# Riding dt's columns on z's projection and spreading short work over the steps of an attention and state-space kernel

## The reference, cut to what matters

```python
q = einsum('dc,bcn->bnd', wq, xf) + bq;  k = ... ;  v = ...          # layer 0, d = 32
x1 = gamma * einsum('bcn,bmn->bcm', v, softmax(q @ k)) + x
u = layernorm(x1 as tokens) * norm_g + norm_b                         # layer 1
zxbcdt = einsum('bld,ed->ble', u, in_w)                               # 772 rows of in_w
z, xBC, dt = zxbcdt[..., :256], zxbcdt[..., 256:768], softplus(zxbcdt[..., -4:] + dt_bias)
xs, B, C = split(silu(causal_conv4(xBC) + conv_b))
state = state * exp(dt_t * A) + (dt_t * x_t) outer B_t;  y_t = state @ C_t + Dp * x_t
y = y * silu(z);  y = y * rsqrt(mean(y * y) + eps) * rms_w
out = y @ out_w.T;  result = x1 + out * gate(mean(out))
```

## Time and profile before

| | |
|---|---|
| median of 3 runs | 3138.42 us (3137.31 to 3141.98) |
| the profiled execution | 3134.2 us |
| its span, first to last instruction | 3132.1 us |
| TensorE busy | 2969.5 us |
| VectorE, ScalarE, GpSimd busy | 2038.2, 1922.7, 2006.3 us |
| mean granted clock of TensorE, share of full speed | 0.982 |

### The profile page before, as it was taken

The page is one execution under the profiler, slowest core; times in us unless marked ns, Lnnn a source line. Parts: engine busy times, 40 slices in busy tenths (PEclk is TensorE's granted clock), DMA queues, the critical chain, the costliest instruction groups (busy, mean ns, idle before and its releaser), DMA issues. The chain is left out here.

```text
span 3132.1 us, 63156 instructions
## 1 busy us (share of the span) xinstructions
PE 2969.5 (95%) x21208; PEld 2322.8 (74%) x21208; DVE 2038.2 (65%) x3417; ACT 1922.7 (61%) x3742; POOL 2006.3 (64%) x3087
## 2 busy tenths in 40 slices
PE   6899999999999999999999999999999999999984
PEld 3767777777777777777777777777778777777763
DVE  5556666666766676676676666676666667676654
ACT  2555666666656666666665666666666666666652
POOL 2446666667756666666776656666676767777763
PEclk9999999999999999999999999999999999999996
DMA  4111111121321121222220122211221011111121
GB/s 123 49 44 33 45 58 54 35 61 40 100 71 65 58 84 48 89 77 70 83 95 30 57 85 65 78 66 64 73 90 36 30 63 62 56 63 50 55 95 67
DMA packets 101970, 200.99 MB, mean 64 GB/s; under 512 B 18480, under 2 KB 41392, under 8 KB 97264
## 3 DMA queue, kind: packets, MB, share of 16 engines
q1 hardware_dynamic: 98192, 195.08, 18.6%
q10 hardware_dynamic: 3456, 1.86, 0.2%
HBM read 131.21 MB, written 64.75 MB: 63 GB/s over the span
## 5 line engine op out<-in xcount | busy, mean ns | idle before, releaser
L723 POOL TENSOR_TENSOR p_lo<-p,p_hi 128x512 f16<-128x512 f32 x1024 | 1219.6, 1198 | 836.8 <-ACT p_hi L886 709.1
L879 ACT ACTIVATE p<-p_et 128x512 f32<-128x512 f32 x1024 | 612.2, 598 | 638.4 <-PE p_et L1138 591.7
L1156 PE MATMUL acc<-v_hi,p_hi 128*128 128x257 f16 x4096 | 955.3, 274 | 4.0 <-DVE work L1464 3.8
L1158 PE MATMUL acc<-v_lo,p_hi 128*128 128x256 f16 x4096 | 952.9, 273 | 0.0
L1420 DVE TENSOR_REDUCE maxes<-p_mx 128x1 f32<-128x1024 f32 x508 | 620.2, 1221 | 500.0 <-PE p_mx L1117 499.8
L886 ACT ACTIVATE p_hi<-p 128x512 f16<-128x512 f32 x1024 | 644.4, 629 | 10.0
L1164 PE MATMUL acc<-v_hi,p_lo 128*128 128x257 f16 x4096 | 623.0, 274 | 16.7 <-POOL p_lo L723 16.7
L1156 PEld LDWEIGHTS acc<-v_hi,p_hi 128*128 128x128 f16 x4096 | 399.8, 98 | 125.0 <-issue 54.6
L1158 PEld LDWEIGHTS acc<-v_lo,p_hi 128*128 128x128 f16 x4096 | 400.9, 98 | 118.6 <-issue 50.4
L1164 PEld LDWEIGHTS acc<-v_hi,p_lo 128*128 128x128 f16 x4096 | 400.0, 98 | 69.9 <-POOL p_lo L723 17.6
L1138 PE MATMUL p_et<-qs,kst 98*128 98x256 f16 x2048 | 393.2, 273 | 12.4 <-ACT p L879 11.7
(11 more groups left out here) (213 smaller groups left out, 4163.5 us busy)
## 6 DMA issues: line engine op xcount, KB each, us to landing
work<-rows_d SPq DMA_DIRECT2D x32, 1024.0 KB, 5.1
xin<-in_x_dram SPq DMA_DIRECT2D x48, 512.0 KB, 5.2
xr<-in_x_dram SPq DMA_DIRECT2D x32, 512.0 KB, 3.7
x_d<-x1c SPq DMA_DIRECT2D x31, 512.0 KB, 3.0
og_d<-og SPq DMA_DIRECT2D x29, 512.0 KB, 2.7
mix_x<-x_d SPq DMA_DIRECT2D x25, 512.0 KB, 4.7
mix_o<-og_d SPq DMA_DIRECT2D x24, 512.0 KB, 5.6
out_dram<-mix_o SPq DMA_DIRECT2D x24, 512.0 KB, 2.8
```

Of the source, the lines that this page charges most:

```text
L723: e.tensor_tensor(p_lo[:, n % RING, :], p32[:, n % P32S, :], p_hi[:, n % RING, :], ALU.subtract).then_inc(lo_pool, 1)
L879: e.activation(p32[:, n % P32S, :], p_et[:, :], ACT.Exp).then_inc(exp_done, 1)
L1156: e.matmul(acc[:, t, 0:C + 1], p_hi[:, r, at:at + P], v_hi[:, 2 * k + kk, 0:C + 1], start=(k == 0 and kk == 0), stop=False)
L1158: e.matmul(acc[:, t, 0:C], p_hi[:, r, at:at + P], v_lo[:, 2 * k + kk, :], start=False, stop=False, skip_group_check=True)
```

## The change

The weights of z and dt lie side by side in `inz_sb`, and a fill of z covers one chunk of 128 tokens with 260 columns, 256 of z and 4 of dt. There are four such fills, at steps 10, 11, 13 and 15. The separate fill of dt is gone. VectorE adds the bias of dt for one chunk at a time, together with z's product. The rest of dt's chain, the decays and their loads are 4 to 5 steps later. `zt` has two buffers. The root mean square's three Newton rounds are spread over steps 23, 24 and 25. `max_parts` stands ahead of `stage_b` and `stage_a` in its step.

```diff
-K_X1T, K_UT, K_DT, K_DAT, K_CUM, K_YT, K_OUT = 3, 9, 10, 21, 23, 30, 0
+K_X1T, K_UT, K_DT, K_DAT, K_CUM, K_YT, K_OUT = 3, 9, 15, 25, 27, 30, 0
-K_Z = (22, 24)
-K_XSB = (25, 27, 28, 29)
+K_Z = (10, 11, 13, 15)
+K_XSB = (26, 27, 28, 29)
...
-        inT_sb = sb("inT_sb", [P, CH, 2 * C + 2 * NST + NH])
+        inT_sb = sb("inT_sb", [P, CH, CONVD])
+        inz_sb = sb("inz_sb", [P, CH, C + NH])
...
-                   (inT_sb[:, :, :], inT.rearrange("(h p) n -> p h n", p=P)),
+                   (inT_sb[:, :, :], inT[:, C:C + CONVD].rearrange("(h p) n -> p h n", p=P)),
+                   (inz_sb[:, :, 0:C], inT[:, 0:C].rearrange("(h p) n -> p h n", p=P)),
+                   (inz_sb[:, :, C:C + NH], inT[:, C + CONVD:C + CONVD + NH].rearrange("(h p) n -> p h n", p=P)),
...
-            def root_mean(g):
-                e.wait_ge(rms_guess, g + 1)
-                newton(rw).then_inc(rms_ready, 1)
+            def root_mean(g, part):
+                if part == 0:
+                    e.wait_ge(rms_guess, g + 1)
+                ins = newton(rw, 1)
+                if part == 2:
+                    ins.then_inc(rms_ready, 1)
...
-                    if K == K_RMS + 1:
-                        root_mean(g)
+                    if K_RMS + 1 <= K < K_RMS + 4:
+                        root_mean(g, K - K_RMS - 1)
...
-                if K == K_DAT - 2:
+                if K == K_DAT - 1:
                     e.wait_ge(dt_ready, g + 1)
                     wait(e, filled, n_filled(("dAT", g - 1, 0)) if g else 0)
                     e.activation(dA16[:, :], dtt[:, 7, :], ACT.Exp).then_inc(dA_done, 1)
...
+                for t in range(QT):
+                    if K == K_Z[t]:
+                        key = ("z", g, t)
                         e.wait_ge(filled, n_filled(key))
+                        wait(e, y_ready, (g - 1) * QT)
+                        e.activation(zt[g % 2][:, t, :], bank(key)[:, 0:C], ACT.Tanh, scale=0.5).then_inc(ztanh_done, 1)
...
-                elif name == "dt":
+                elif name == "z":
                     e.wait_ge(uT_done, 2 * g + 2)
                     o = begin(key)
-                    for t in range(QT):
-                        for h in range(CH):
-                            mm = e.matmul(o[:, t * NH:(t + 1) * NH], uT[:, h, t * P:(t + 1) * P],
-                                          inT_sb[:, h, C + CONVD:C + CONVD + NH], start=(h == 0), stop=(h == CH - 1))
-                    mm.then_inc(filled, 1)
-                elif name == "z":
-                    o = begin(key)
-                    for t in range(2):
-                        for h in range(CH):
-                            mm = e.matmul(o[:, t * C:(t + 1) * C], uT[:, h, (2 * i + t) * P:(2 * i + t + 1) * P],
-                                          inT_sb[:, h, 0:C], start=(h == 0), stop=(h == CH - 1))
+                    for h in range(CH):
+                        mm = e.matmul(o[:, 0:C + NH], uT[:, h, i * P:(i + 1) * P], inz_sb[:, h, :],
+                                      start=(h == 0), stop=(h == CH - 1))
                     mm.then_inc(filled, 1)
...
+                for t in range(QT):
+                    if K == K_Z[t]:
+                        key = ("z", g, t)
+                        e.wait_ge(ztanh_done, QT * g + t + 1)
+                        if t == 0:
+                            wait(e, dt_ready, g)
+                        v.tensor_tensor(dtt[:, 0, t * NH:(t + 1) * NH], bank(key)[:, C:C + NH], dtb[:, :], ALU.add)
+                        v.scalar_tensor_tensor(zt[g % 2][:, t, :], zt[g % 2][:, t, :], 1.0, bank(key)[:, 0:C],
+                                               ALU.add, ALU.mult).then_inc(zs_done, 1)
+                if K == K_DT:
+                    e.drain()
+                    v.scalar_tensor_tensor(dtt[:, 1, :], dtt[:, 0, :], -1.0, dtt[:, 0, :], ALU.mult, ALU.max)\
+                        .then_inc(dtabs_ready, 1)
+                    v.tensor_scalar(dtt[:, 3, :], dtt[:, 0, :], 0.0, None, ALU.max)
+                if K == K_DT + 2:
+                    e.wait_ge(dtexp_done, g + 1)
+                    v.tensor_scalar(dtt[:, 4, :], dtt[:, 2, :], 2.0, None, ALU.add)
...
+                    if K % STEPS == (K_PARTS if n >= STEPS else K_PARTS_FIRST) and n // STEPS + 1 < NHALF:
+                        max_parts(n // STEPS + 1)
                     if h < NHALF and K % STEPS == (K_QR if n >= STEPS else K_QR_FIRST):
                         query_rows(h)
```

More of the change, by code:

```diff
@@ L130, in fills_at @@
             out += [("uT", A, 0), ("uT", A, 1)]
-        if K == K_DT:
-            out += [("dt", A, 0)]
         if K == K_DAT:
@@ L136, in fills_at @@
             out += [("cumT", A, 0)]
-        for r in range(2):
-            if K == K_Z[r]:
-                out += [("z", A, r)]
+        for t in range(QT):
+            if K == K_Z[t]:
+                out += [("z", A, t)]
         for c in range(QT):
@@ L268, in conv_attention_mamba_kernel @@
         yT = work[:, 4096:5120].rearrange("p (h n) -> p h n", h=CH)
-        zt = work[:, 5120:6144].rearrange("p (t c) -> p t c", t=QT)
+        zt0 = work[:, 5120:6144].rearrange("p (t c) -> p t c", t=QT)
         dAb = work[:, 6144:8192]
+        zt = [zt0, sb("zt1", [P, QT, C])]
         xin = [sb(f"xin{r}", [P, CH, BLK]) for r in range(2)]
@@ L756, in decays, with newton @@
                                 ALU.mult).then_inc(Sd_ready, 1)
-            def newton(w):
-                for _ in range(3):
+            def newton(w, steps=3):
+                for _ in range(steps):
                     e.tensor_tensor(w[:, 1, :], w[:, 3, :], w[:, 3, :], ALU.mult)
@@ L951, in stage_a @@
                         e.activation(th[:, m % 2, :], cv, ACT.Tanh).then_inc(tanh_done, 1)
-                for r in range(2):
-                    if K == K_Z[r]:
-                        key = ("z", g, r)
+                for t in range(QT):
+                    if K == K_Z[t]:
+                        key = ("z", g, t)
                         e.wait_ge(filled, n_filled(key))
-                        wait(e, y_ready, g * QT)
-                        e.activation(zt[:, 2 * r:2 * r + 2, :], bank(key)[:, :].rearrange("p (t c) -> p t c", t=2),
-                                     ACT.Tanh, scale=0.5).then_inc(ztanh_done, 1)
+                        wait(e, y_ready, (g - 1) * QT)
+                        e.activation(zt[g % 2][:, t, :], bank(key)[:, 0:C], ACT.Tanh, scale=0.5).then_inc(ztanh_done, 1)
                 for c in range(QT):
@@ L1531, in stage_a @@
                         v.memset(xbc[:, :, 0:HALO], 0.0).then_inc(halo_done, 1)
-                for r in range(2):
-                    if K == K_Z[r]:
-                        key = ("z", g, r)
-                        e.wait_ge(ztanh_done, 2 * g + r + 1)
-                        v.scalar_tensor_tensor(zt[:, 2 * r:2 * r + 2, :], zt[:, 2 * r:2 * r + 2, :], 1.0,
-                                               bank(key)[:, :].rearrange("p (t c) -> p t c", t=2), ALU.add, ALU.mult)\
-                            .then_inc(zs_done, 1)
+                for t in range(QT):
+                    if K == K_Z[t]:
+                        key = ("z", g, t)
[13 more added lines that the diff above has]
+                    v.tensor_scalar(dtt[:, 4, :], dtt[:, 2, :], 2.0, None, ALU.add)
+                    e.drain()
+                    v.reciprocal(dtt[:, 5, :], dtt[:, 4, :])
+                    e.drain()
+                    v.tensor_tensor(dtt[:, 4, :], dtt[:, 2, :], dtt[:, 5, :], ALU.mult).then_inc(dtz_ready, 1)
                 if K == K_DAT:
@@ L1634, in step @@
                 if s < G:
-                    if K % STEPS == (K_PARTS if n >= STEPS else K_PARTS_FIRST) and n // STEPS + 1 < NHALF:
-                        max_parts(n // STEPS + 1)
                     if K == K_BN:
```

31 lines of the change are left out of this document (6 added, 25 removed).

## The result

The changed kernel takes 3171.52 us (median of 4 runs, 3169.69 to 3174.78) against 3137.86 of the kernel before on the same chip (4 runs, 3133.5 to 3141.98): a ratio of 1.0108, 95% interval 1.0093 to 1.0123. It is slower by 34 us, where 37 us less were forecast. The profiled execution has a span of 3172.7 us, 40.6 more than before; about 7 of these 40.6 are spread between executions, since the profiled one lies 3.7 us under the median before and 3.3 over it after.

The account below looks back on a forecast made before the run. TensorE's list was taken to set the pace. The terms, from -52.7 for dt's fill to +17 for new waits at steps 22 to 26, sum to -37 us: 3097 profiled, 3101 median; 8-in-10 range 3076 to 3122.

Parts of the forecast that it names:

- an end stage longer by over 8 us: Sign of being wrong: the stage behind the last tile grows by more than 8 us.
- the shorter slots: Sign of being right: slots without projections become shorter by about 1.2 us.
- The fill of dt: Step 10: removing dt's separate fill takes 1.70 us a slot, 52.7 us in all, off TensorE.
- Dt's matmuls are hidden: Rival at dt's fill: weights load under other matmuls, only 2 us are won, 3152 us; chance 0.02.
- The fills of z: Four fills for two on TensorE: 1.8 us for added columns, 3.2 us for changes between matmul kinds.
- Steps 10 to 21: Steps 10 to 15 save 2.7 us in all through shorter waits; steps 17 to 21 cost 3 us.
- The 3 us at steps 17 to 21: TensorE waits 0.1 us a slot for the exponential at step 21, since dt's VectorE work delays a tap.
- Steps 22 to 26: New wait for the exponential at step 26: 10 us, plus 7 in special slots, less 9.0 of v fill.
- GpSimd as 0: Steps 18 to 26: moved series and split rounds keep every `p_lo` in time, so GpSimd costs 0.
- GpSimd becomes the bound: Rival at steps 18 to 27: series and rounds come too late, about 3205 us; chance 0.05.
- The end: Behind the last tile: dt's later chain through series, load and scan costs 2 us, from -6 to +8.
- The decay rows: Made 4 steps later; slack between load landing and scan falls from 21 to 10 us, so hidden.

Follow-up runs that it names:

- e13: Changed kernel with two of a slot's 32 `p_lo` (tiles 24 and 25) replaced by a memset of 4 columns: 3114.81 us.
- e2: Changed kernel with the three root mean square rounds in one piece again at step 23: 3171.94 us.
- e10: e8 with the three root mean square rounds in one piece again, at step 22: 3191.4 us.
- e7: Changed kernel with the last block kept in its old order (own dt fill, z at steps 22 and 24): 3157.47 us.
- e5: Changed kernel with the root mean square's guess at step 21, last square at step 20, rounds at steps 22 to 24: 3120.94 us.
- e8: Changed kernel with both the guess at step 21 and the old order for the last block: 3111.23 us.
- e11: e8 with `max_parts` behind `stage_b` and `stage_a` again, as in the kernel before: 3097.56 us.
- e14: Changed kernel with only `max_parts` put behind `stage_b` and `stage_a` again: 3133.11 us.

## Why the prediction was wrong

The bound, the terms for TensorE's own work and the place of the new wait were right. What failed is the length of VectorE's short operations at steps 22 to 24, the clock behind a wait, and the price of the chain in the end stage. One of the prediction's signs of being wrong came, an end stage longer by over 8 us; of its signs of being right, the shorter slots did not (slot 25 takes 89 us).

**The fill of dt: right.** Step 10 takes 27.2 us less in 30 slots with a z chunk of 0.87 in dt's place, so dt cost 1.78 us a slot; 1.70 was counted. *Dt's matmuls are hidden* is refuted: by that rule step 10 would have become longer. The prediction also says that at 25 ns a matmul "the change would take only some 12 us off"; that is dt's term alone (31 x 0.4), and its whole sum would then be about +3. The section of the Trainium skill that it takes the 25 ns from (page TensorE: Matmul & The Clock Gate, section Back-to-back issue gap) gives them for a matmul by itself, and says that in a stream with a weight load for each matmul the load counts too; each of dt's 512 had one, and the trace has 0.106 us.

**The fills of z: right.** Four chunks cost 3.51 us a slot against 3.45 for two fills before, 1.7 us in all; 5.0 was counted. VectorE's 256-column passes took 0.41, as the earlier trace rows let expect.

**Steps 10 to 21: right, some us too dear.** `cb` waits for z's product 3.7 us in 3 slots, and the idle time of steps 15 and 16 went from 7.6 us to 0.5. The 3 us at steps 17 to 21 did not come (0.4 us, once).

**Steps 22 to 26: this step failed.** The place was right (the scores of step 26, for the exponential, behind Tanh and third tap), the direction too, and the size wrong: 17 us of new waits less 9 won, where 75 were measured. The count set the third tap's end 6.1 us behind the start of step 22. With the two `p_lo` away (e13) it is 6.2, and TensorE's waits for the exponential at step 26 come to 9.4 us, close to the 10 that I counted; steps 22 to 27 then take 455.0 us, 15 above the 439.7, where I had counted 8. What the count left out is that the 0.17 us of a small operation of VectorE (the guess's rows of before, above) hold only while no `p_lo` runs beside it. The trace of before showed this in other places, where I took no row: the subtraction that makes `mparts`, 2 elements a partition, took 0.44 us on average there and 0.16 in slot 25. I moved `max_parts` in the list as a harmless 0.9 us and did not ask what it and the series would put side by side.

**The clock: no term at all.** In 13 of the 30 slots TensorE ran at half the clock behind this wait, 3.4 us in twelve and 6.8 in one. There it made a wait of 1.9 us cost 3.6.

**GpSimd as 0: right here for the wrong reason.** I argued that splitting the rounds keeps `p_lo` in time. The time is the same without it (e2), because another wait hid it; in e10, where that wait is gone, my argument holds and is worth 80 us. The rival *GpSimd becomes the bound* did not come as priced, its rounds stayed at 0.35 us each; but GpSimd did cost the time, through VectorE.

**The end: too small.** +14 (e7 gives it back: -14.0; e5 to e8: -9.7), counted as +2 within -6 to +8. That dt comes late behind z and the convolution was right; the chain that I priced behind it, through the decays' load and the scan, was not the one that ended last. The 7.8 us between scan and `cb` were no room to be eaten: the two are still 6.6 us apart. What TensorE waited for is what I named in one sentence and gave no price: root mean square and output of the block before, behind GpSimd's series. The rounds start 12.8 us later, the output fill 10.1, and at half the clock it takes 2.8 more.

**The decay rows: right.** In slot 25 the load is issued at 2498.51 and read at 2514.59, 16 us later.

On the span, the forecast of -37 and the measured +40.6 differ by 77.6 us: 67 in steps 22 to 27 (75 against 8), 12 in the end stage, and 2 the other way in all the rest.

## What to carry to other kernels

When work leaves the bounding engine, list for the stretch it left every operation of the other engines up to the next thing awaited, and price a small one by what its kind costs where it meets GpSimd, not by a place where it stood alone: an operation of 0.17 us on VectorE can cost what is left of GpSimd's operation beside it. The mean of the group is no guard if all of it stood alone, as the guess's did before (0.17); the subtraction's 0.44 was the hint. An order that looks neutral (which of two short pieces of VectorE work goes first) was worth 38 us, more than half of it in the steps concerned through the clock, and the same edit was worth 80 us or nothing (the rounds) and 50 or 4 (the guess), depending on what else was late; so parts of a change are worth testing one by one and again on the repaired version. The last block, behind which nothing is hidden, may need an order of its own.

## What the runs showed of the hardware

A `tensor_scalar` or cast of VectorE over a few elements in SBUF takes 0.16 to 0.17 us alone and up to 1.15 us in the changed kernel where a `p_lo` of GpSimd has begun before it (1.10 for the guess's first operation in slot 25 of e11), and ends when that one does. So does the subtraction of `max_parts`, which has two SBUF inputs: 0.16 against up to 1.15. The taps, which read PSUM and one SBUF tensor, are not touched, 755 ns on average before and after, and the small reduction ahead of `max_parts`' other three takes 161 in both, beside a `p_lo` or not. The Trainium skill has the rule (page SBUF — State Buffer, section Who interferes with whom): VectorE's second port pair is GpSimd's only one, copy, cast and `tensor_scalar` can take both pairs, whoever comes first holds it for the whole instruction and the other one waits fully, and reductions never contend. The traces agree where they bear on it, with the numbers above: the `tensor_scalar` waits and the reduction doesn't. The other order is in the traces too: where VectorE's scan `lt` (two SBUF inputs) had begun, the `p_lo` beside it took up to 2.08 us in the changed kernel, with a median of 1.16 over all.

After an idle time of 1.91 us at step 26 of slot 25 the granted clock stood at half for 3.35 us, and something like it came in 13 of 30 slots. The length of the wait alone doesn't decide it: in slots 4, 6 and 8 the same wait was 1.99, 2.03 and 3.11 us and the clock stayed at full, and at step 24 in e14 it fell behind a wait of 1.75 us (slot 6) and not behind 1.95 and 1.99 (slots 11 and 19).
